# Perceiver layer on one Trainium2 core: tail products in two fp32r parts, set-up over more banks, the last group's rest in two token parts, the context's lower parts made by POOL

## Chip, cores and metric

One core of one Trainium2 chip runs the whole program in one launch. The metric is the device time of that launch in microseconds, the median of several runs.

## The reference, cut to what matters

64 batches of 32 queries (256 wide) look at 257 context rows (192 wide) with 16 heads of 64; then a self-attention of 16 heads of 16 over the 32 queries of a batch, then a gated feed-forward whose mixing takes the row before. All three are residual.

```python
x = x + xattn(layernorm(x), ctx)      # its own LN inside; q = xn@Wq, k,v = ctx@Wkv; softmax; @Wo + bo
x = x + attn(layernorm(x))            # LN; qkv = h@W_qkv + b; softmax over 32 keys; @W_proj + b
x = x + ffn(layernorm(x))             # xr, xk mix x and the row before; sigmoid(xr@Wr.T) * (relu(xk@Wk.T)**2 @ Wv.T)
```

## The kernel before

**Groups.** The 64 batches go in 8 groups of 8 (256 tokens, two tiles of 128). A group's work has three kinds. *Pre* work (XT, Q0 to Q3, K0 to K11) makes, for the next group, the queries already multiplied by the key weights (`qk_h`, `qk_l`, `qk_t`), so that scores are taken against the context itself. *Batch* work is the cross-attention of one batch `j`. *Post* work (OT0, OT1, WO0, WO1, T2, QT, KT, SC, VR, PT, PV, T4, PJ, T3, FR, FK, FV) is everything behind the cross-attention, for the group before.

**Batch work.** CT transposes the context on TensorE into `aux`; ACT rounds it to an upper part `cT_h` (fp32r) and DVE subtracts to get the lower part `cT_l`. S0 to S3 (L661) are four score tiles of five fp32r products each. DVE masks them and takes the row extremes (L1142), ACT makes the exponentials and their sums (L928), DVE the reciprocals (R0, R1, L1148), POOL normalises (N0, N1, L491). P0 and P1 transpose the probabilities (L670) into `probT`; ACT copies them to `prT` (L937), then to the fp32r upper part `prT_h` (U0, U1, L945), and POOL subtracts to get `prT_l` (L0, L1, L356). CU (ACT, L952) and CL (DVE, L348) make the same two parts of the context's first 128 channels, `c_h` and `c_l`. AC (`weigh`, L685 to L695) multiplies: the context's last 64 channels, the tail, in plain fp32 from `prT` and `cx_in` (four matmuls of 256 columns, L685), and the first 128 channels in six fp32r matmuls of 512 columns (L691, L692, L695) into `ac_main`. It waits for `prT` before the tail, for `prT_h` and `c_l` before the first four of the six, and for `prT_l` before the last two. ACT copies `ac_main` to `acm`, DVE `ac_tail` to `act_`.

**Order.** Each engine runs through a list written out by hand (`PE_ORDER`, `ACT_ORDER`, `DVE_ORDER`, `POOL_ORDER`), the same for all groups; what a group does not have is left out by `stream`. An engine issues its list in order, so a wait holds all that stands behind it. After the last group the `*_CLOSING` lists do the post work of group 7, all 256 tokens in each step, over eight PSUM banks.

**Set-up.** SP loads x, all of Wq (1 MB), the key weights, the context's last rows, small columns, the three feed-forward weights, the mask, four contexts and the rest. TensorE transposes x (XT), then the key weights (WK0 to WK3) and the feed-forward weights (F0 to F2) between Q0 to Q3, and then K0 to K10 over two pairs of PSUM banks, each waiting for the split before the last; the first score waits for 10 of the 12 splits. POOL's first work waits for all eight weight loads, and ACT's first for all seven small loads.

**Layer norm** (`layer_norm` on DVE) is a chain of small instructions linked by a semaphore: statistics, their sum, a seed by integer shift, three Newton steps of three links each, and the normalising pass.

## Time and profile before

| | us |
|---|---|
| median of 3 runs (902.51 to 904.21) | 902.88 |
| the profiled execution | 905.87 |
| its span, first to last instruction | 903.4 |
| PE busy of the span | 822.6 |
| DVE, ACT, POOL busy | 579.5, 549.5, 430.7 |

A busy time is the union of an engine's instructions. TensorE's are pipelined with modelled ends, so the distance between two starts tells more of its rate than the duration of one. In timeline rows the columns are the start in us from the span's start, the duration in us, engine, line, operation, what is written and read, shape and count; in brackets the engine's idle time before it and what ended it.

### The profile page before, as it was taken

What the parts mean: (1) busy time and instruction counts of PE and PEld (TensorE: products, weight loads), DVE (VectorE), ACT (ScalarE), POOL (GpSimd) and SP (SyncE); (2) the same over time, 40 slices, a digit from 0 to 9 for tenths busy, and PEclk for the clock granted to TensorE, in tenths of its full rate; (3) what the DMA queues carried; (4) which work ended last, traced back from release to release, by engine and by line L of the source; (5) the groups of instructions that cost most, each with busy time, mean ns of one, the idle gap of its engine ahead of it and who ended that gap; (6) DMA issues with size and microseconds to landing.
All of it is one profiled execution on the core that took longest, in us unless ns stands there. A gap on an engine that the chain in (4) does not pass through costs nothing.

```text
span 903.4 us, 20097 instructions
## 1 busy us (share of the span) xinstructions
PE 822.6 (91%) x7414; PEld 641.3 (71%) x7414; DVE 579.5 (64%) x1674; ACT 549.5 (61%) x1338; POOL 430.7 (48%) x661
## 2 busy tenths in 40 slices
PE   5699989998999989998999989998999999897653
PEld 3487758785878758786878768785878768684532
DVE  2553475769576775778576775778576756682344
ACT  1566865688467865677467865677467864673111
POOL 1036733755256723755266724755266724764001
PEclk9889999999999999999999999999999999999767
DMA  7301110001000110102010110002000110000000
GB/s 208 123 12 48 25 48 13 25 25 50 22 25 25 28 56 12 26 24 64 9 25 25 36 48 13 25 24 71 1 25 25 37 36 13 25 12 24 1 1 12
DMA packets 49232, 30.49 MB, mean 34 GB/s; under 512 B 22896, under 2 KB 48304, under 8 KB 49136
## 3 DMA queue, kind: packets, MB, share of 16 engines
q1 hardware_dynamic: 49136, 29.22, 11.9%
q8 instruction: 59, 0.97, 0.5%
q14 instruction: 37, 0.30, 0.1%
HBM read 26.85 MB, written 2.10 MB: 32 GB/s over the span
## 4 chain that ended last, share of the span: by engine, by line
PE 67%; DVE 14%; issue 7%; POOL 6%; ACT 5%; SPq 1%; DMA 1%; POOLq 0%; DVEq 0%; ACTq 0%
PE score L661 15%; PE post L755 5%; PE pre L573 5%; DVE qk_t L1123 5%; PE probT L670 4%; PE ac_tail L685 4%; POOL prT_l L356 4%; PE post L764 3%; DVE qk_l L1118 3%; PE ac_main L691 3%; PE ac_main L695 3%; PE aux L624 2%; PE ac_main L692 2%; PE post L738 2%; PE post L744 2%
## 5 line engine op out<-in xcount | busy, mean ns | idle before, releaser
L491 POOL TENSOR_SCALAR pr<-pr,rsum,poison 128x257 f32<-128x257 f32 x256 | 166.6, 660 | 233.6 <-DVE rsum L1148 233.5
L356 POOL TENSOR_TENSOR prT_l<-prT,prT_h 128x512 fp32r<-128x512 f32 x128 | 169.1, 1324 | 126.6 <-ACT prT_h L945 126.6
L928 ACT ACTIVATE pr<-sm,nmx 128x257 f32<-128x257 f32 x256 | 129.8, 509 | 83.8 <-DVE nmx L1142 83.4
L1142 DVE CUSTOM_DVE_ANT_0 sm<-score,mbias 128x257 f32<-128x257 f32 x256 | 106.2, 422 | 85.4 <-PE score L661 68.5
L937 ACT ACTIVATE prT<-probT 128x512 f32<-128x512 f32 x128 | 75.6, 590 | 44.9 <-PE probT L670 44.5
L661 PE MATMUL score<-cT_h,qk_h 128*128 128x258 f32 x256 | 89.6, 350 | 13.2 <-DVE qk_t L1123 12.9
L945 ACT ACTIVATE prT_h<-prT 128x512 fp32r<-128x512 f32 x128 | 80.7, 630 | 1.1
L670 PE MATMUL probT<-ident,pr 128*128 128x128 f32 x512 | 77.7, 274 | 3.4 <-POOL pr L491 2.6
L661 PE MATMUL score<-cT_h,qk_t 128*128 128x258 f32 x256 | 73.5, 287 | 0.0
L661 PE MATMUL score<-cT_l,qk_h 128*128 128x258 f32 x256 | 73.1, 285 | 0.0
L661 PE MATMUL score<-cT_h,qk_l 128*128 128x258 f32 x256 | 73.1, 285 | 0.0
L685 PE MATMUL ac_tail<-prT,cx_in 128*64 128x256 f32 x512 | 70.2, 395 | 3.0 <-ACT prT L937 2.3
L661 PE MATMUL score<-cT_l,qk_t 128*128 128x258 f32 x256 | 72.9, 285 | 0.0
L670 PEld LDWEIGHTS probT<-ident,pr 128*128 128x128 f32 x512 | 60.1, 140 | 14.1 <-POOL pr L491 7.2
L661 PEld LDWEIGHTS score<-cT_h,qk_h 128*128 128x128 f32 x256 | 48.8, 191 | 25.2 <-DVE qk_t L1123 12.5
L573 PE MATMUL pre<-xnT,wq 128*128 128x256 f32 x256 | 64.0, 395 | 0.5 <-ACT xnT L891 0.5
L1132 DVE TENSOR_TENSOR cT_l<-aux,cT_h 128x512 fp32r<-128x512 f32 x64 | 44.0, 688 | 27.3 <-ACT cT_h L920 27.0
L691 PE MATMUL ac_main<-prT_h,c_h 128*128 128x512 f32 x128 | 57.8, 451 | 0.0
L573 PEld LDWEIGHTS pre<-xnT,wq 128*128 128x128 f32 x256 | 48.4, 199 | 6.4 <-issue 0.7
L1148 DVE RECIPROCAL rsum<-ssum 128x2 f32<-128x2 f32 x128 | 20.5, 160 | 49.2 <-ACT pr L928 49.1
L685 PEld LDWEIGHTS ac_tail<-prT,cx_in 128*64 128x64 f32 x512 | 31.8, 137 | 28.0 <-issue 11.0
L692 PE MATMUL ac_main<-prT_h,c_l 128*128 128x512 f32 x128 | 51.0, 398 | 0.0
(260 smaller groups left out, 2024.5 us busy)
## 6 DMA issues: line engine op xcount, KB each, us to landing
cx_in<-in_ctx_dram SPq DMA_DIRECT2D x64, 192.0 KB, 2.4
cx_in<-in_ctx_dram SPq DMA_DIRECT2D x64, 64.0 KB, 2.3
xn<-in_x_dram SPq DMA_DIRECT2D x8, 256.0 KB, 3.4
xb<-in_x_dram SPq DMA_DIRECT2D x8, 256.0 KB, 3.5
out_dram<-yo SPq DMA_DIRECT2D x8, 256.0 KB, 2.7
wq<-in_L_xattn_Wq_dram SPq DMA_DIRECT2D x1, 1024.0 KB, 5.1
wo<-in_L_xattn_Wo_dram SPq DMA_DIRECT2D x1, 1024.0 KB, 7.6
wqkv<-in_L_attn_W_qkv_dram SPq DMA_DIRECT2D x1, 768.0 KB, 8.8
```

Of the source, the lines that this page charges most:

```text
L356: eng.tensor_tensor(prT_l[:, :, cut], prT[:, :, cut], prT_h[:, :, cut], ALU.subtract).then_inc(prob_lower, 1)
L491: last = pool.tensor_scalar(p, p, rsum[:, j % 2, t:t + 1], poison[:, 0:1], ALU.mult, ALU.mult)
L573: last = pe.matmul(pre[:, i * TOK:(i + 1) * TOK], wq[:, k, (2 * n + i) * P:(2 * n + i + 1) * P], xnT[:, k, :], start=(k == 0), stop=(k == 1))
L661: last = pe.matmul(score[t % 2][:, 0:NK + 1], q[:, j, tile], c, start=(i == 0), stop=(i == len(products) - 1))
L670: last = pe.transpose(probT[:, m * 256 + i * P:m * 256 + (i + 1) * P], pr[j % 2][:, 2 * half + i, m * P:(m + 1) * P], ident[:])
L685: pe.matmul(ac_tail[r * 64:r * 64 + 64, 0:TOK], cx_in[j % NCTX][:, m, P:DC], by_pair[:, :, r, :], start=(m == 0), stop=(m == 1))
L691: pe.matmul(ac_main[:], c_h[j % 2][:, m, :], prT_h[:, m, :], start=(m == 0), stop=False)
L692: pe.matmul(ac_main[:], c_l[j % 2][:, m, :], prT_h[:, m, :], start=False, stop=False)
L928: act.activation(pr[j % 2][:, t, :], sm[:, t % 2, :], ACT.Exp, bias=nmx[:, j % 2, t:t + 1], scale=-1.0, accum_out=ssum[:, j % 2, t:t + 1]) ...
L937: act.activation(prT[:, :, half * 256:(half + 1) * 256], probT[:].rearrange("p (m c) -> p m c", m=2), ACT.Copy).then_inc(probT_copied, 1)
L945: act.activation(prT_h[:, :, cut], prT[:, :, cut], ACT.Copy).then_inc(prob_upper, 1)
L1142: dve.tensor_tensor_reduce(sm[:, t % 2, :], score[t % 2][:, 0:NK], mbias[:], DH ** -0.5, BIG, ALU.add, ALU.min, nmx[:, j % 2, t:t + 1]).th ...
```

## The change

**AC.** `c_h` and `c_l` become one tile `c_hl` of 128 x 2 x 384: upper part of the first 128 channels, then upper and lower parts of the tail side by side (TAILS, 128 wide), then the lower part of the first 128. The tail is no longer plain fp32: four fp32r matmuls of 512 columns with TAILS as stationary operand write `ac_tail`, its rows 0 to 63 for the upper and 64 to 127 for the lower part. The wait for `prT` alone goes; all of AC waits for `prT_h` and `c_lower`, and the two last pairs for `prT_l`. ACT copies rows 64 to 127 to `act_low` ahead of its copy of `ac_main`; DVE adds the halves in two instructions. CL, now two subtractions, is made by POOL. CU rounds 192 columns a row where it took 128. `prT` is written again once `prT_l` is made, not once AC is done; that wait moves to `prT_h`.

```diff
 def weigh(g, j):
-    pe.wait_ge(probT_copied, n)
-    for m in range(2):
-        by_pair = prT[:, m, :].rearrange("p (n r x) -> p n r x", r=2, x=2 * NQ)
-        for r in range(2):
-            pe.matmul(ac_tail[r * 64:r * 64 + 64, 0:TOK], cx_in[j % NCTX][:, m, P:DC], by_pair[:, :, r, :],
-                      start=(m == 0), stop=(m == 1))
     pe.wait_ge(c_lower, g * GB + j + 1)
     pe.wait_ge(prob_upper, n)
+    c = c_hl[j % 2]
     for m in range(2):
-        pe.matmul(ac_main[:], c_h[j % 2][:, m, :], prT_h[:, m, :], start=(m == 0), stop=False)
-        pe.matmul(ac_main[:], c_l[j % 2][:, m, :], prT_h[:, m, :], start=False, stop=False)
+        pe.matmul(ac_main[:], c[:, m, UPPER], prT_h[:, m, :], start=(m == 0), stop=False)
+        pe.matmul(ac_main[:], c[:, m, LOWER], prT_h[:, m, :], start=False, stop=False)
+        pe.matmul(ac_tail[:], c[:, m, TAILS], prT_h[:, m, :], start=(m == 0), stop=False)
     pe.wait_ge(prob_lower, n)
     for m in range(2):
-        last = pe.matmul(ac_main[:], c_h[j % 2][:, m, :], prT_l[:, m, :], start=False, stop=(m == 1))
+        pe.matmul(ac_main[:], c[:, m, UPPER], prT_l[:, m, :], start=False, stop=(m == 1))
+        last = pe.matmul(ac_tail[:], c[:, m, TAILS], prT_l[:, m, :], start=False, stop=(m == 1))
 def context_lower(eng, g, j):
-    eng.tensor_tensor(c_l[j % 2][:], cx_in[j % NCTX][:, :, 0:P], c_h[j % 2][:], ALU.subtract).then_inc(c_lower, 1)
+    eng.tensor_tensor(c[:, :, DC:2 * P], src[:, :, P:DC], c[:, :, P:DC], ALU.subtract)
+    eng.tensor_tensor(c[:, :, LOWER], src[:, :, 0:P], c[:, :, UPPER], ALU.subtract).then_inc(c_lower, 1)
-LOWER_ON_DVE = ("CL",)
+LOWER_ON_DVE = ()
 def weighed(g, j):   # ACT
+    after(act, act_copied, g * GB + j)
+    act.activation(act_low[:], ac_tail[64:128], ACT.Copy).then_inc(tail_lower, 1)
     act.activation(acm[...], ac_main[...], ACT.Copy).then_inc(acm_copied, 1)
 def weighed(g, j):   # DVE
-    dve.wait_ge(ac_done, g * GB + j + 1)
-    dve.tensor_copy(act_[...], ac_tail[:, 0:TOK]...).then_inc(act_copied, 1)
+    dve.wait_ge(tail_lower, g * GB + j + 1)
+    for r in range(2):
+        last = dve.tensor_tensor(own, upper[:, :, r], lower[:, :, r], ALU.add)
+    last.then_inc(act_copied, 1)
```

**Orders.** Each engine gets three lists: for group 0, for groups 1 to 6, and for group 7 with its own rest. The middle ones differ in places only; AC stands on average a little later behind its P1.

```diff
 PE_ORDER = (
-    "S0:0 S1:0 CT:1 OT0 S2:0 S3:0 OT1 LV0 S0:1 P0:0 CT:2 LV1 WO0 XT S1:1 WO1 S2:1 S3:1 P1:0 CT:3 Q0 S0:2 AC:0 T2 S1:2 "
...
-    "S1:7 S2:7 FK AC:5 S3:7 P0:6 FV P1:6 K0 K2 AC:6 P0:7 K4 P1:7 K6 LT K8 AC:7 CT:0 K10").split()
+    "S0:0 CT:1 S1:0 OT0 S2:0 S3:0 OT1 CT:2 LV0 P0:0 LV1 S0:1 WO0 S1:1 P1:0 WO1 S2:1 XT AC:0 S3:1 Q0 CT:3 S0:2 T2 S1:2 "
...
+    "S1:7 FR S2:7 P0:6 FK AC:5 S3:7 P1:6 FV K0 K2 AC:6 P0:7 LT K4 P1:7 K6 CT:0 K8 AC:7 K10").split()
 DVE_ORDER = (
...
-    "CT:7 AC:4 S1:6 S2:6 R1:5 M1 S3:6 CL:5 S0:7 R0:6 FR CL:6 S1:7 R1:6 S2:7 SG AC:5 R0:7 S3:7 FV K0 CL:7 K1 R1:7 K2 K3 "
-    "AC:6 K4 K5 LT K6 K7 K8 K9 CT:0 AC:7 K10 K11").split()
+    "R0:7 R1:7 AC:5 K0 K1 K2 K3 LT K4 K5 AC:6 K6 CT:0 K7 K8 K9 K10 K11 AC:7").split()
 POOL_ORDER = (
...
+    "CT:1 XB CL:0 CL:1 N0:0 CT:2 N1:0 L0:0 L1:0 N0:1 N1:1 CT:3 X1 N0:2 CL:2 L0:1 L1:1 N1:2 CT:4 N0:3 L0:2 L1:2 N1:3 W0 W1 "
...
```

**Last group.** The post work of group 7 is done for tokens 0 to 127 (names with .0) and 128 to 255 (.1) apart, the first part in two PSUM banks and the second in six, with a second set of scratch tiles in `wq`. OT0.0, OT1.0 and WO.0 stand ahead of AC:7. The output is stored in two parts.

```diff
-PE_CLOSING = (
-    "OT0 OT1 WO0 WO1 T2 KT QT SC0 VR SC1 PT0 PT1 PV T4 PJ T3 FR FK FV").split()
+PE_LAST = (
...
+    "S2:7 S3:7 P1:6 AC:5 FR FK P0:7 AC:6 FV OT0.0 P1:7 OT1.0 WO.0 LT.1 AC:7 OT0.1 T2.0 OT1.1 QT.0 KT.0 WO.1 SC.0 VR.0 "
+    "T2.1 QT.1 KT.1 SC.1 VR.1 PT.0 PV.0 T4.0 PJ.0 PT.1 PV.1 T4.1 PJ.1 T3.0 T3.1 FR.0 FK.0 FR.1 FV.0 FK.1 FV.1").split()
+DVE_LAST = (
...
+    "B1.0 B2.0 B3.0 B4.0 B5.0 LT.1 B6.0 AC:7 B7.0 B8.0 B9.0 B10.0 B11.0 KM.0 WO.1 B0.1 B1.1 B2.1 B3.1 B4.1 B5.1 B6.1 B7.1 "
+    "B8.1 B9.1 B10.1 B11.1 SC.0 VR.0 KM.1 SM.0 SC.1 VR.1 SM.1 PJ.0 C0.0 C1.0 C2.0 C3.0 C4.0 C5.0 PJ.1 C6.0 C0.1 C7.0 C8.0 "
+    "C1.1 C9.0 C2.1 C10.0 C3.1 C11.0 C4.1 C5.1 C6.1 C7.1 C8.1 C9.1 C10.1 C11.1 M1.0 FR.0 M1.1 SG.0 FR.1 FV.0 SG.1 FV.1").split()
```

**Set-up.** SP loads the two small columns that XT needs and the key weights ahead of Wq, and Wq in two halves; the feed-forward weights come later and are transposed in group 0 (F0 to F2). K0 to K11 of group 0 (H0 to H11) run over four pairs of banks; score tile 0 waits for 4 of the splits, tile 1 for 6, tile 2 for 10, tile 3 for 12. Waits for all weights and all small loads move to where they are used. A two-column ACT copy stands ahead of the first real one.

```diff
-SETUP = "WK0 Q0 WK1 F0 Q1 WK2 F1 Q2 WK3 F2 Q3".split()
+SETUP = "WK0 WK1 XT WK2 WK3 Q0 LEFT Q1 CT0".split()
+PE_FIRST = (
+    "H0 G2 H2 S0:0 H4 H6 CT:1 G3 H8 H10 S1:0 S2:0 LV0 S3:0 CT:2 S0:1 P0:0 S1:1 LV1 P1:0 S2:1 S3:1 CT:3 F0 S0:2 S1:2 S2:2 "
...
+QK_SETUP_BANKS = [(score[0], score[1]), (post, probT), (ac_main, ac_tail), (post, probT), (ac_main, ac_tail), (post, pre)]
+FIRST_USE_0 = {0: 4, 1: 6, 2: 10, 3: 12}
```

**Layer norm.** -0.5 times the variance is made once, so a Newton step is two links (one `scalar_tensor_tensor` for each token tile, then one for both) and each link is a job of its own in DVE's list.

## Rows read from the trace of the kernel before

**Rows 1.** The page's first part: busy us, share of the span, instructions.
```profile
PE 822.6 (91%) x7414; PEld 641.3 (71%) x7414; DVE 579.5 (64%) x1674; ACT 549.5 (61%) x1338; POOL 430.7 (48%) x661
```

**Rows 2.** Windows, us: length, busy of PE, PEld, DVE, ACT, POOL, clock, DMA.
```profile
0.00:50.00 50.00, 31.73 (x189) 22.79 (x190) 21.99 (x69) 18.71 (x37) 3.34 (x17) 0.90 0.51 149
427.00:528.00 101.00, 98.36 (x921) 77.61 (x921) 71.94 (x208) 67.67 (x167) 54.06 (x81) 1.00 0.12 30
730.00:826.00 96.00, 88.09 (x785) 68.66 (x785) 57.75 (x176) 55.98 (x145) 54.68 (x79) 0.98 0.08 23
826.00:904.00 78.00, 44.67 (x420) 32.42 (x420) 28.71 (x66) 12.82 (x25) 5.79 (x6) 0.76 0.01 4
```

**Rows 3.** PE's timeline: the first score of group 1 and of group 7.
```profile
123.71 0.36 PE L661 MATMUL score<-cT_h,qk_h 128*128 128x258 f32 x1 [1.37 <-DVE qk_t L1123]
...
730.55 0.36 PE L661 MATMUL score<-cT_h,qk_h 128*128 128x258 f32 x1 [1.37 <-DVE qk_t L1123]
```

**Rows 4.** PE's timeline: one AC and the score behind it.
```profile
405.55 1.08 PE L685 MATMUL ac_tail<-prT,cx_in 128*64 128x256 f32 x8
406.56 0.50 PE L691 MATMUL ac_main<-prT_h,c_h 128*128 128x512 f32 x1
406.90 0.39 PE L692 MATMUL ac_main<-prT_h,c_l 128*128 128x512 f32 x1
...
408.06 0.28 PE L661 MATMUL score<-cT_h,qk_h 128*128 128x258 f32 x1
```

**Rows 5.** Lines by form: count, busy us, mean ns; idle before.
```profile
L348 DVE TENSOR_TENSOR c_l<-cx_in,c_h 128x256 fp32r<-128x256 f32 x64 | 34.6, 551 | 0.3
L1123 DVE TENSOR_TENSOR qk_t<-score,qk_t 64x512 fp32r<-64x512 f32 x32 | 22.0, 689 | 1.7 <-ACT qk_t L911 1.0
L1160 DVE COPY act_<-ac_tail 128x256 f32<-128x256 f32 x64 | 26.5, 414 | 10.4 <-PE ac_main L695 10.0
L911 ACT ACTIVATE qk_t<-score 64x512 fp32r<-64x512 f32 x32 | 18.9, 592 | 2.2 <-PE score L610 1.9
L356 POOL TENSOR_TENSOR prT_l<-prT,prT_h 128x512 fp32r<-128x512 f32 x128 | 169.1, 1324 | 126.6 <-ACT prT_h L945 126.6
L506 POOL TENSOR_TENSOR xb<-xb,bo_row 128x256 f32<-128x256 f32 x16 | 11.3, 729 | 0.0
```

**Rows 6.** Timeline of the stretch K0 to K10, a group's last 16 us.
```profile
514.86 1.52 DVE L348 TENSOR_TENSOR c_l<-cx_in,c_h 128x256 fp32r<-128x256 f32 x1
...
528.26 0.36 PE L661 MATMUL score<-cT_h,qk_h 128*128 128x258 f32 x1 [1.35 <-DVE qk_t L1123]
```

**Rows 7.** Timeline of the set-up.
```profile
7.93 1.08 PE L556 MATMUL pre<-ident,xn 128*128 128x128 f32 x4 [7.93 <-DVE xn L1099]
...
12.77 1.02 ACT L891 ACTIVATE xnT<-pre,cols 128x256 f32<-128x256 f32 x2 [2.38 <-DMA bcol<-in_L_attn_b_qkv_dram]
...
13.93 3.75 PE L573 MATMUL pre<-xnT,wq 128*128 128x256 f32 x8 [0.55 <-ACT xnT L891]
...
44.98 0.55 PE L661 MATMUL score<-cT_h,qk_h 128*128 128x258 f32 x1 [3.40 <-DVE qk_t L1123]
```

**Rows 8.** Timeline behind the last AC, from its copy to the store.
```profile
825.95 0.60 ACT L956 ACTIVATE acm<-ac_main 128x512 f32<-128x512 f32 x1 [3.78 <-PE ac_main L695]
...
835.54 3.69 PE L755 MATMUL ac_tail<-wo,qT 128*128 128x256 f32 x16 [1.29 <-ACT qT L988]
...
847.65 1.12 PE L556 MATMUL score<-ident,hn 128*128 128x128 f32 x4 [4.97 <-DVE hn L1099]
...
867.60 1.05 POOL L517 TENSOR_TENSOR sc<-sc,rs 128x512 f32<-128x512 f32 x1 [22.97 <-DVE rs L1211]
...
880.24 0.69 DVE L1223 TENSOR_TENSOR x<-post,xb 128x512 f32<-128x512 f32 x1 [11.28 <-PE post L799]
...
894.77 3.35 DVE L1250 RECIPROCAL sc<-sc 128x512 f32<-128x512 f32 x1
...
900.89 0.38 SPq L414 DMA_DIRECT2D out_dram<-yo  x1
```

888 lines of the change are left out of this document (503 added, 385 removed), and 40 rows, old and new, of tables (ACT_FIRST, ACT_LAST, ACT_ORDER, DVE_FIRST).

## The prediction

> **What bounds the kernel now.** I read the page's busy times first: TensorE is busy for 91% of the span, no other engine for more than 64% [rows 1]. The windows say where the rest lies. A middle group holds TensorE for 98.4 of its 101 us, with DVE at 71.9, ACT at 67.7 and POOL at 54.1 [rows 2]; there TensorE's own work is the time, and the groups repeat to a hundredth: from 123.71 to 730.55 six of them take 101.14 each [rows 3]. The two ends are another matter. In the first 50 us TensorE is busy for 31.7; behind the last AC it is busy for 44.7 of 78 at a mean clock of 0.76 [rows 2]. Three sizes follow: a start of 123.7 us up to group 1, six groups of 101.1, a last group of 95.4 up to the end of its last AC at 825.9, and a rest of 77.5 up to 903.4 [rows 3, 8].
>
> **AC.** The fp32 tail takes 1.01 us (405.55 to 406.56) and the six fp32r matmuls 1.50: the first 0.34, the other five 0.23 each [rows 4]. The new AC is ten such matmuls, 2.31 at 0.23, or 2.42 with a first one of 0.34. The dearer first is what the turn from fp32 to fp32r costs, and there is one such turn before and after. So 2.51 becomes 2.31 to 2.42; an fp32 piece ahead is also overlapped by the turn, so I take 0.2 saved (bounds 0.09 and 0.28). That is **1.6 us a group**, 13 in all.
>
> The other engines pay. ACT copies 64x512 more (0.59 [rows 5]) and rounds 192 columns for 128 (some 0.1); that is 8 x 0.69 = 5.5, so 73 of 100. DVE loses CL (8 x 0.55 = 4.4) and has two additions for one copy, each like that copy's 0.41 (so 8 x 0.41 = 3.3 more), and stays near 71. POOL gains CL: 128x256 at 0.73 as its additions, and the 128x128 part, of which no row tells: between nothing and the same 0.73; 1.32 for 512 elements and 0.73 for 256 [rows 5] lead on to 0.43 for 128, which I take. So 1.16 a batch, 9.3 a group (5.8 to 11.7), 63 of 100. None passes TensorE, so in the sum these cost nothing; their cover is TensorE's queue, and the first rival below says what happens if it is gone.
>
> What is queued behind the moved wait: AC now starts when `prT_h` is made, where the tail needed `prT` alone, and what lies between AC's start and the wait for `prT_l` shrinks from 1.01 + 0.96 to 1.39 us. But `prT` may be rewritten without waiting for the last AC, and the lists put AC:0 some 4.5 us of TensorE work behind P1:0 where it had 2.8, while copy, rounding and subtraction take 0.6 + 0.6 + 1.3 (the last in [rows 5]). I cost it at zero, with 0.4 us per AC as the other end.
>
> **The stretch of K0 to K10.** At every group's end the first score waits 1.35 us for DVE's last split [rows 6], and DVE's `c_l` in that stretch takes 1.52 us, against a mean of 0.55, beside POOL's `prT_l`. It leaves DVE's chain there, one extra addition (0.41) comes in: 1.1 us of the wait go. I take **1.0 us a group**; nothing at worst, 2 at best with the other waits of that stretch. The GPSIMD Engine Reference of the Trainium skill (Specifications) says that POOL's SBUF interface is shared with VectorE and that contention comes with two-SBUF-input instructions of DVE; by that rule the collision goes for good, since the new additions have one operand in PSUM. By the row alone it could move to another DVE instruction, and the 1.0 would be zero, 7 us in all.
>
> **Middle groups:** 101.1 - 1.6 - 1.0 = 98.5, six times 2.6 is **-15.6** (between 0 and -27).
>
> **Set-up and group 0.** x is normalised by 7.9, and then `xnT` waits for small loads until 12.77, 2.38 us of it for the DMA alone [rows 7]. The new order has the two columns and the key weights ahead of Wq's megabyte. The key weights should be there near 7, so WK0, WK1 and XT run from 7 to 11, where TensorE had XT and then stood idle, and Q0 starts near 13.5 as before (13.93 [rows 7]), but behind four WK instead of one. F0 to F2 leave (2 us at the low clock) and return in group 0 at full clock (1.3). Two Q's at 3.75 [rows 7] bring H0 to 21.5. DVE's 12 splits are 16 instructions of 0.69 [rows 5], 11 us; with a mask, CT:1 and some 3 us of waits between they end near 37. Before, the tenth came at 44.98, after a wait of 3.40 [rows 7], and the last two 1.4 later, at 46.4: 9 us, and 2 more as score tiles, CT:1 and LV0 now run between the K's, where they followed. From -11, plus 1.3 for F0 to F2, -1.6 for AC, -1.0 for the stretch at the end: **-12** (between -6 and -16). The waits for weights stand at LV0, near 37; the loads land before 31 now and the bytes are the same, so they cost nothing.
>
> **Last group up to its last AC.** It has no next queries to make, and TensorE is busy for 88.1 of 96 [rows 2]. AC saves 1.6; OT0.0, OT1.0 and WO.0 come in. OT takes 7.7 us (9.6 from 825.95 to 835.54, less 0.6 and 1.3 for the copies [rows 8]); on half the columns 3.8 if the columns set the time, 7.7 if the instructions do. I take 4.6, near the columns. WO.0 takes 3.6, as one of the two. 88.1 - 1.6 + 8.2 = 94.7, and some waits remain: **0** (between -3 and +5).
>
> **The rest.** The second token part sets the end; I walk the milestones [rows 8] with halved work:
> - 825.95 to 835.54, 9.6: now the tail's copy and additions first (+1.0), half of OT (4.6), T2.0, QT.0 and KT.0 in between (2.4), copies: 8.6.
> - to 847.65, 12.1: one WO (3.6), not two, one addition, a layer norm of 3.0 where it was 4.4 (12.1 less two WO and 0.4; now one tile, and 11 links for 14): 7.1.
> - to 867.60, 20.0: T2, hT, QT, KT on half the columns 3.5, KM 2.4, then DVE's own queue: SM.0, SC.1, VR.1, SM.1, some 5.4 at 0.69 for 512 and 0.41 for 256 elements [rows 5]: 11.3. DVE is the bound here, as it carries both parts.
> - to 880.24, 12.6: one POOL product (1.05), one PT, PV, T4, PJ behind those of part 0: 6.8.
> - to 894.77, 14.5: layer norm 3.0 with 1.5 of the other part's links, T3, mixing, FR: 10.3.
> - to 900.89, 6.1: the reciprocal of 3.35 is halved to 1.7, the last product and sum as well: 3.0. Then the store, 2.5.
>
> Together 49.6. I add 5 for the clock and for in-order queues, since the chip had TensorE at 0.76 here and more but shorter gaps may leave it there: 54.5, **-23** (between -15 and -28).
>
> **Sum:** 903.4 - 12 - 15.6 - 0 - 23 = 852.8 for the span, 855.3 for the execution (2.5 around the span). The profiled execution lies 3.0 above the median of the runs shown, so the median should be **852 us**, 5.6% less.
>
> **Rivals.**
> 1. *POOL in the way, slower than before.* CL stands in POOL's list ahead of N and L, which P and AC wait for, in order. If all of it (1.1 us) lay on the path of each batch, 8.8 us a group, seven groups 62, the sum would be 852 + 62 = 914; it decides from 0.9 us a batch. For it: POOL is 1.3 to 1.8 times slower than DVE at this shape [rows 5], and with TensorE at 98% every new wait counts. Against: POOL stands idle 47 of 101 us, and its L waits for ACT's `prT_h` for most of that [rows 5]. The same reference's table (Engine selection) says not to give GpSimd an elementwise instruction of two inputs, some 2x slower than VectorE there, which speaks against this part of the change; twice DVE's 0.41 and as much in proportion for the tail would make CL an estimated 1.3, POOL 65 of 100, and the point of decision nearer, the sum the same. 3%.
> 2. *The middle groups gain nothing.* The later start of AC and ACT's 0.6 us before each `acm` copy give back 2.6 us a group as new waits: 852 + 15.6 = 868. For it: 0.3 us per AC is enough. Against: AC stands later. 17%.
> 3. *The clock stays low at both ends.* Work in short pieces leaves TensorE at 1.2 GHz: some 20 us of its work in the rest take 6 more, the start 4 more: 862. For it: both halves of the rest still wait for DVE. 15%.
> 4. *More goes.* TensorE's idle time left in a middle group (2.6 [rows 2], less the 1.0 taken) goes as well, and AC saves 0.28 (0.6 a group): 96.3 a group, 13 us more: 839. For it: the lists are new for the new work. 12%.
> 5. *The change does nothing in the middle and little at the ends*, as both are bound by loads and DVE: within 0.2% of before, 1%.
> The forecast itself has 52%.
>
> **How the numbers follow.** Cases 2 to 4 reach 839 to 868; the unknowns of the terms move the forecast by some 10 either way. I take 838 to 872 as the range that holds the time 8 times in 10. 0.2% is about what a measurement of this kernel tells from no change. Faster by more has 0.96, same 0.01, slower 0.03.
>
> **What would show it.** In the profile after: AC in ten matmuls 2.3 to 2.4 us from start to start; the first scores of groups 1 and 7 at 111.7 and 702.7, 98.5 apart per group; the wait ahead of each group's first score below 0.5 us; the fourth score of batch 0 near 39; POOL busy for some 63% of a group; 54 to 55 us from the last AC to the end. I am wrong if TensorE waits for `prT_h`, `prT_l` or `pr` at most ACs (rival 1 or 2), or if the rest takes over 62 us, which would put the error in DVE's queue between the two parts.

## The result and the profile after

The changed kernel takes 894.94 us (median of 9 runs, 892.30 to 898.48) where the kernel before, in the same comparison, takes 901.89: a ratio of 0.9926, with a 95% interval of 0.9905 to 0.9947. That is 0.7% faster. I had said 852 us, in a range of 838 to 872, so the sign was right and the size far off. (One profiled execution of an experiment, that of e1_setup_order, ran at a granted clock of 0.85 throughout and took 948.66 us; it is left out of that kernel's time.)

Its profiled execution spans 890.3 us. First the page's first part, to be read against [rows 1]; columns as there.

```profile
PE 808.1 (91%) x7279; PEld 658.7 (74%) x7279; DVE 587.8 (66%) x1729; ACT 600.1 (67%) x1423; POOL 480.0 (54%) x792
```

TensorE lost 14.5 us of work, ACT and POOL gained some 50 each. The windows, to be read against [rows 2], show the stages. Columns: stretch, its length, busy time of PE, PEld, DVE, ACT and POOL with the instruction counts, clock, DMA share, GB/s.

```profile
0.00:50.00 50.00, 32.50 (x190) 20.99 (x191) 22.17 (x65) 17.59 (x37) 4.52 (x21) 0.90 0.52 149
427.00:527.00 100.00, 97.03 (x893) 80.15 (x891) 72.22 (x210) 73.92 (x175) 59.68 (x97) 1.00 0.12 31
724.32:836.27 111.95, 95.10 (x866) 77.72 (x866) 61.12 (x186) 63.10 (x156) 61.50 (x96) 0.98 0.08 21
836.27:890.29 54.02, 32.90 (x429) 25.66 (x428) 32.39 (x91) 15.64 (x42) 5.46 (x7) 0.86 0.02 6
```

A middle group still keeps TensorE busy 97% of the time. The last group, up to the end of its last AC, is 112 us long for 95 us of work. Next, the first scores of group 1, of a middle group and of group 7 in TensorE's timeline, the rows that answer to [rows 3] (start, length, instruction, and in brackets the idle time before it and what ended it).

```profile
124.55 0.39 PE L786 MATMUL score<-cT_h,qk_h 128*128 128x258 f32 x1
...
424.44 0.39 PE L786 MATMUL score<-cT_h,qk_h 128*128 128x258 f32 x1 [0.81 <-DVE qk_t L1270]
...
724.32 0.39 PE L786 MATMUL score<-cT_h,qk_h 128*128 128x258 f32 x1 [0.79 <-DVE qk_t L1270]
```

So six groups take (724.32 - 124.55) / 6 = 99.96 us each. One AC in the same view, with the score behind it, answers to [rows 4].

```profile
483.38 0.48 PE L812 MATMUL ac_main<-prT_h,c_hl 128*128 128x512 f32 x1
483.69 0.39 PE L813 MATMUL ac_main<-prT_h,c_hl 128*128 128x512 f32 x1
483.93 0.40 PE L814 MATMUL ac_tail<-prT_h,c_hl 128*128 128x512 f32 x1
...
485.76 0.28 PE L786 MATMUL score<-cT_h,qk_h 128*128 128x258 f32 x1
```

From 483.38 to 485.76 are 2.38 us: 0.31 for the first matmul and 0.23 for each of the nine others. And the lines by form of the whole span for the work that the other engines took over, to be read against [rows 5] (count, busy us, mean ns; idle before).

```profile
L419 POOL TENSOR_TENSOR c_hl<-cx_in,c_hl 128x128 fp32r<-128x128 f32 x64 | 29.6, 462 | 13.5 <-ACT c_hl L1073 13.4
L420 POOL TENSOR_TENSOR c_hl<-cx_in,c_hl 128x256 fp32r<-128x256 f32 x64 | 47.0, 734 | 0.0
L1079 ACT ACTIVATE act_low<-ac_tail 64x512 f32<-64x512 f32 x64 | 38.2, 596 | 23.0 <-PE ac_tail L818 21.7
L1302 DVE TENSOR_TENSOR act_<-ac_tail,act_low 64x256 f32<-64x256 f32 x128 | 52.7, 412 | 4.6 <-ACT act_low L1079 3.7
```

The four stretches of the prediction's sum, in us:

| stretch | before | forecast | after | off by |
|---|---|---|---|---|
| start to the first score of group 1 | 123.7 | -12 | 124.55 (+0.8) | 12.8 |
| six middle groups | 606.8 | -15.6 | 599.8 (-7.1) | 8.5 |
| last group to the end of its last AC | 95.4 | 0 | 112.0 (+16.6) | 16.6 |
| the rest | 77.5 | -23 | 54.0 (-23.5) | -0.5 |
| sum | 903.4 | -50.6 | 890.3 (-13.1) | 37.5 |

The 13.1 us of the last line are more than the 6.7 us that the ratio gives. The 903.4 belong to an execution of 905.87 us, slower than all nine of this comparison, and the 890.3 to the fastest of its nine (892.30). The start is one part that moves from one execution to the next: in e5_before_cl_pool below, whose lists are those of before up to there, the first score comes at 40.91 where it is at 44.98 in before, as TensorE waits 0.96 and not 2.50 us for its first load (`acm`), and the Q matmuls behind it reach their full pitch sooner. So the +0.8 of the first line is known to some 4 us only, which does not make a -12 of it.

The rest came as forecast, the other three did not. The experiments take them one by one. All are held against the kernel before, run on the same chip beside them; stages come from one profiled execution of each.

### The profile page after: what moved, and what is told of

It reads as the page before. It is cut to its first block, busy times and chain, and to the rows that moved or that the text cites. A ratio compares the mean times of both kernels' runs of the same rounds, so it can differ in the third digit from the quotient of the medians.

```text
span 890.3 us, 20369 instructions
## 1 busy us (share of the span) xinstructions
PE 808.1 (91%) x7279; PEld 658.7 (74%) x7279; DVE 587.8 (66%) x1729; ACT 600.1 (67%) x1423; POOL 480.0 (54%) x792
## 4 chain that ended last, share of the span: by engine, by line
PE 66%; DVE 16%; ACT 6%; issue 6%; POOL 3%; SPq 1%; DMA 1%; DVEq 0%; POOLq 0%; ACTq 0%
PE score L786 14%; PE post L872 5%; DVE qk_t L1270 4%; PE pre L671 4%; PE probT L797 4%; PE post L881 3%; PE aux L730 2%; PE ac_main L812 2%; DVE qk_l L1265 2%; PE ac_main L817 2%; PE ac_tail L818 2%; PE ac_tail L814 2%; PE ac_main L813 2%; DVE kM L1350 2%; PE post L852 2%
## 5 line engine op out<-in xcount | busy, mean ns | idle before, releaser
L571 POOL TENSOR_SCALAR pr<-pr,rsum,poison 128x257 f32<-128x257 f32 x256 | 141.8, 564 | 157.7 <-DVE rsum L1295 157.6
L786 PE MATMUL score<-cT_h,qk_h 128*128 128x258 f32 x256 | 92.5, 362 | 19.1 <-DVE qk_t L1270 11.4
L786 PE MATMUL score<-cT_h,qk_l 128*128 128x258 f32 x256 | 72.7, 284 | 0.0
L786 PE MATMUL score<-cT_l,qk_t 128*128 128x258 f32 x256 | 72.7, 284 | 0.0
L812 PE MATMUL ac_main<-prT_h,c_hl 128*128 128x512 f32 x128 | 55.7, 435 | 4.0 <-POOL c_hl L420 2.6
L671 PE MATMUL pre<-xnT,wq 128*128 128x256 f32 x232 | 55.5, 382 | 0.6 <-ACT qT L1014 0.6
L1302 DVE TENSOR_TENSOR act_<-ac_tail,act_low 64x256 f32<-64x256 f32 x128 | 52.7, 412 | 4.6 <-ACT act_low L1079 3.7
L1079 ACT ACTIVATE act_low<-ac_tail 64x512 f32<-64x512 f32 x64 | 38.2, 596 | 23.0 <-PE ac_tail L818 21.7
L1039 ACT ACTIVATE cT_h<-aux 128x512 fp32r<-128x512 f32 x64 | 38.2, 597 | 21.8 <-PE aux L730 21.8
L817 PE MATMUL ac_main<-prT_l,c_hl 128*128 128x512 f32 x128 | 50.3, 393 | 1.0 <-POOL prT_l L428 1.0
L786 PEld LDWEIGHTS score<-cT_l,qk_h 128*128 128x128 f32 x256 | 49.0, 192 | 2.3
L872 PE MATMUL post<-wo,qT 128*128 128x256 f32 x224 | 50.6, 379 | 0.0
```

The lines of the kernel that those rows point to most:

```text
L571: last = pool.tensor_scalar(p, p, rsum[:, j % 2, t:t + 1], poison[:, 0:1], ALU.mult, ALU.mult)
L671: last = pe.matmul(bank[:, i * TOK:(i + 1) * TOK], wq[:, k, (2 * n + i) * P:(2 * n + i + 1) * P], xnT[:, k, :], start=(k == 0), stop=(k == 1))
L786: last = pe.matmul(score[t % 2][:, 0:NK + 1], q[:, j, tile], c, start=(i == 0), stop=(i == len(products) - 1))
L812: pe.matmul(ac_main[:], c[:, m, UPPER], prT_h[:, m, :], start=(m == 0), stop=False)
L817: pe.matmul(ac_main[:], c[:, m, UPPER], prT_l[:, m, :], start=False, stop=(m == 1))
L872: last = pe.matmul(bank[:, 0:DM], qT[:, k, w * P:(w + 1) * P], wo[:, k, :], start=(k == 0), stop=(k == NPAIR - 1))
```

## The experiments

### The order of the split stretch

Where did the set-up's 12 us go? The first H products stand where I had them (H0 at 21.50, forecast 21.5), but the fourth score of batch 0 comes at 48.77, not near 39. In the changed kernel's timeline two rows tell of it, TensorE's first score and ACT's copy of the context of batch 1.

```profile
29.95 0.58 PE L786 MATMUL score<-cT_h,qk_h 128*128 128x258 f32 x1 [4.41 <-DVE qk_t L1270]
```

```profile
35.88 0.60 ACT L1039 ACTIVATE cT_h<-aux 128x512 fp32r<-128x512 f32 x1 [7.41 <-PE aux L730]
```

TensorE's list has S0:0, which waits for four splits, ahead of H4 and H6, which could have run. ACT's list has CT:1 ahead of H4. CT:1 stands in TensorE's list behind H6, so ACT stands idle for 7.4 us although H4's products were ready 2.6 us before that ended (33.3), and DVE behind it stands for 6.6. Only this order was changed:

```diff
-PE_FIRST  "H0 G2 H2 S0:0 H4 H6 CT:1 G3 H8 H10 ..."
+PE_FIRST  "H0 G2 H2 H4 G3 CT:1 S0:0 H6 H8 H10 ..."
-ACT_FIRST "H0 H1 H2 G2 H3 CT:1 H4 H5 H6 G3 H7 ..."
+ACT_FIRST "H0 H1 G2 H2 H3 H4 H5 G3 CT:1 H6 H7 ..."
-DVE_FIRST "H0 H1 H2 H3 CT:1 H4 S0:0 H5 H6 ..."
+DVE_FIRST "H0 H1 H2 H3 H4 H5 CT:1 S0:0 H6 ..."
```

> Kernel after with only the hand-written order of the split stretch changed: the second products H4 ahead of the first score, ACT copies H4 and H5 ahead of the context of batch 1, DVE likewise. Theory 1 (the in-order queues cost the start its gain): TensorE stood 4.4 us ahead of the first score with H4 and H6 behind it, ACT stood 7.4 us for the context while H4's products were ready. Then the fourth score of batch 0 comes at 41 to 43 us instead of 48.8, group 1's first score at 117 to 119 instead of 124.6, and the kernel is 6 to 8 us shorter than after (about 888). Rival (DVE's splits and the low clock set the stretch, whatever the order): the fourth score stays within 1.5 us of 48.8 and the time within 2 us of after (893 to 897).

Measured: 888.00 us (three executions), ratio 0.9847 (0.9799 to 0.9895). In its profiled execution the fourth score comes at 41.66 and group 1's first score at 119.78. The same order in c1_both below, at a granted clock of 0.98, gives 41.10 and 117.20, both inside what theory 1 said. TensorE's first, second and fourth score in c1_both:

```profile
30.80 0.39 PE L788 MATMUL score<-cT_h,qk_h 128*128 128x258 f32 x1 [0.91 <-DVE qk_t L1272]
...
35.83 0.39 PE L788 MATMUL score<-cT_h,qk_h 128*128 128x258 f32 x1
...
41.10 0.36 PE L788 MATMUL score<-cT_h,qk_h 128*128 128x258 f32 x1
```

The idle time ahead of the first score falls from 4.41 to 0.91 and 7.7 us are gone by the fourth. So a few items in three in-order lists cost 7.4 us of the start (124.55 to 117.20), of the 12.8 by which the forecast missed it. The loads were in time for this: TensorE's first H product came at 21.50, as forecast.

### The last group: the early part, and the order

The last group has two new things: OT0.0, OT1.0 and WO.0 ahead of its last AC, and lists of its own. First the early part alone was moved behind AC:7, on all engines.

```diff
 PE_LAST
-"... P0:7 AC:6 FV OT0.0 P1:7 OT1.0 WO.0 LT.1 AC:7 OT0.1 ..."
+"... P0:7 AC:6 FV P1:7 LT.1 AC:7 OT0.0 OT1.0 WO.0 OT0.1 ..."
 DVE_LAST
-"... AC:6 WO.0 B0.0 B1.0 B2.0 B3.0 B4.0 B5.0 LT.1 B6.0 AC:7 B7.0 ..."
+"... AC:6 LT.1 AC:7 WO.0 B0.0 B1.0 B2.0 B3.0 B4.0 B5.0 B6.0 B7.0 ..."
```

> Kernel after with the first token part's OT0.0, OT1.0, WO.0 and the links B0.0 to B6.0 moved behind the last AC on all engines; nothing else. In after the last group up to its last AC takes 112.0 us and the rest 54.0. Theory (the early work only moved, its 8.6 us of TensorE lie on the path wherever they stand): the last group 103 to 104, the rest 61 to 63, sum within 1.5 us of after. Rival A (early work in the way of AC:6 and AC:7, adding waits): last group below 102, rest at most 60, 3 us or more shorter. Rival B (early work fills gaps): last group above 106, sum 3 us or more longer.

Measured: 901.76 us, 0.9995 (0.9977 to 1.0014). The last group shrinks by only 2.0, from 112.0 to 110.0, and the rest grows from 54.0 to 66.6. Rival B is right: the early part fills gaps and is worth 10.5 us between the two profiled executions, and some 6 by the ratios (0.9995 against 0.9926). Then the 17 us of gaps come from elsewhere, and the next kernel keeps the early part out and runs the group in the middle groups' order.

```diff
-PE_LAST = "S0:0 CT:1 S1:0 OT0 S2:0 OT1 S3:0 S0:1 CT:2 WO0 ..."
+PE_LAST = PE_ORDER without the jobs for a next group, LT as LT.0 LT.1, then the closing jobs
```

The same was done to the lists of ACT, DVE and POOL.

> As e2_no_early, but the batch part of the last group runs in the order written for the middle groups (less the jobs for a next group) on all four engines. Theory (the last group's own lists are what leaves TensorE waiting 17 us there, the middle order leaves about 3): last group 91 to 96 us, rest 61 to 63, the kernel 5 to 10 us shorter than e2_no_early and than after. Rival (what waits there is the missing work for a next group, so any order leaves the gaps): last group 102 to 104 as in e2_no_early, time the same.

Measured: 889.61 us, 0.9863 (0.9836 to 0.9891). Last group 96.8, rest 65.9. The rest is as long as in e2_no_early (66.6) and longer than the theory had it. The order alone is worth 13.2 us in the last group against e2_no_early, with the same instructions. TensorE's idle time there falls from 18.8 to 10.8 us, and its busy time from 91.1 to 86.0; the granted clock is 0.98 where it was 0.95, so the waits were in part paid for twice. The waits of TensorE (who waited for whom: us in total, times, longest) in the last group, first of the changed kernel:

```profile
PE probT L797 <- POOL pr L571: 3.0, 2, 2.1
PE score L786 <- DVE nmx L1289: 1.4, 2, 1.3
PE post L913 <- ACT kM L1136: 1.4, 1, 1.4
PE aux L730 <- DMA cx_in<-in_ctx_dram: 1.3, 2, 0.8
```

and of e3_last_mid:

```profile
PE ac_main L814 <- DVE act_ L1304: 3.7, 2, 2.0
PE post L647 <- DVE hn L1240: 1.9, 2, 1.0
PE aux L737 <- DVE spread L1312: 1.3, 1, 1.3
```

In the changed kernel there are eighteen such rows, of which the four largest are shown, for every kind of work. Probabilities, scores, contexts and post jobs all come a little late, which fits lists that are ordered badly from start to end. With the middle order there are ten rows, of which three are shown: the waits for POOL's `pr`, `prT_l` and `c_hl` and for the DMA are gone, that for the row extremes `nmx` falls from 1.4 to 0.3, and 5.0 of what is left stand in the last 11 us of the group, behind DVE.

Then the early part was put back into this order.

```diff
 PE_LAST (middle order)
-"... P1:6 FV AC:6 P0:7 LT.0 LT.1 P1:7 CT:0 AC:7 OT0.0 OT1.0 WO.0 ..."
+"... S1:7 LT.0 ... P1:6 FV OT0.0 AC:6 OT1.0 P0:7 WO.0 P1:7 LT.1 CT:0 AC:7 ..."
```

> As e3_last_mid (the last group's batch part in the middle groups' order), with the first token part's OT0.0, OT1.0, WO.0 and B0.0 to B6.0 put back among its last batches: OT0.0 and OT1.0 around AC:6, WO.0 behind P0:7. In e3 the last group took 96.8 us and the rest 65.9. Theory (the early part fills the last group's gaps, in e2 against after it brought 8 us net, and the order was what cost): last group 100 to 103, rest 54 to 56, the kernel 6 to 9 us shorter than e3, about 882. Rival (OT0.0, OT1.0 now delay AC:6 and AC:7 by what they take and their waits; no gap is left in the middle order): last group 105 or more, time as e3.

Measured: 889.72 us, 0.9833 (0.9810 to 0.9856). The last group takes 101.1 as the theory had it, but the rest 62.2 and not 54 to 56. So nothing clear is gained on e3: 0.9833 against 0.9863, with intervals that overlap. POOL's and DVE's timelines show why:

```profile
822.24 1.29 POOL L430 TENSOR_TENSOR prT_l<-prT,prT_h 128x512 fp32r<-128x512 f32 x1 [3.14 <-ACT prT_h L1068]
823.49 1.44 POOL L593 TENSOR_TENSOR xb<-xb,bo_row 128x256 f32<-128x256 f32 x2
```

```profile
825.02 0.42 DVE L1328 TENSOR_TENSOR x<-pre,xb 128x256 f32<-128x256 f32 x1 [9.70 <-issue]
...
827.03 1.16 DVE L1312 TENSOR_TENSOR spread<-aux,seqm 32x128 f32<-32x128 f32 x4
828.22 0.16 DVE L1249 SCALAR_TENSOR_TENSOR lw<-lw 128x1 f32<-128x1 f32 x1
828.30 0.84 DVE L1304 TENSOR_TENSOR act_<-ac_tail,act_low 64x256 f32<-64x256 f32 x2
```

POOL makes `xb` behind the last `prT_l`; DVE's addition for the first part waits for it, 9.7 us idle; and `spread` and the last AC's additions, for which the second part's OT waits, stand behind that addition. Again no engine is busy and a list holds it up.

### Both ends together, and the end mended

c1_both is e8_mid_early with the split stretch of e1_setup_order.

> e8_mid_early together with the order of e1_setup_order. Theory (the two ends don't touch): both gains add, e1's fourth score at 41 to 42 and group 1's first score at 117 to 119.8, then six groups of 99.9, last group and rest as in e8_mid_early: 6 us shorter than e8, about 876. Rival (group 0 gives the start's gain back, as it waits for weights or other engines there): group 1's first score at 122 or later and the time that of e8.

Measured: 880.01 us, 0.9728 (0.9707 to 0.9748). Group 1's first score comes at 117.20, the groups take 99.95, last group and rest 101.2 and 62.4 as in e8. The two ends do not touch: 9.7 us less than e8 by the medians and 6.5 by the profiled spans, of which 6.8 lie ahead of group 1; 6 were expected. c2_both mends the lists at the end of the last group:

```diff
 POOL_LAST "... L0:7
-L1:7 XB.0
+XB.0 L1:7
 DVE_LAST
-"... AC:6 WO.0 B0.0 B1.0 B2.0 B3.0 B4.0 B5.0 LT.1 B6.0 CT:0 AC:7 ..."
+"... AC:6 LT.1 WO.0 B0.0 B1.0 B2.0 B3.0 AC:7 B4.0 B5.0 B6.0 CT:0 ..."
 PE_LAST
-"... FV OT0.0 AC:6 OT1.0 P0:7 WO.0 P1:7 LT.1 CT:0 AC:7 ..."
+"... FV AC:6 OT0.0 P0:7 OT1.0 P1:7 WO.0 LT.1 CT:0 AC:7 ..."
```

ACT's list follows TensorE's.

> c1_both with the end of the last group mended: in the rest of e8 and c1 the second OT waits behind DVE's x addition for the first part, which waited for POOL's xb behind the last prT_l, with the last AC's additions and the spread queued behind it (last group and rest 101.2 and 62.2 us, where after has 112.0 and 54.0). Here POOL makes XB.0 before the last prT_l, DVE makes the spread ahead of that addition and the last AC's additions after four links of the norm, WO.0 stands behind P1:7 and OT1.0 behind P0:7. Theory: last group 100 to 102, rest 54 to 57, the kernel 5 to 8 us shorter than c1, 872 to 875. Rival (the second part's end is set by DVE's and ACT's work on the first part wherever its start lies): rest 60 or more, 878 or more.

Measured: 875.53 us, 0.9706 (0.9674 to 0.9738). Its windows of the last group and the rest:

```profile
716.01:818.76 102.75, 94.01 (x866) 77.57 (x866) 58.26 (x183) 63.30 (x156) 60.89 (x96) 0.98 0.09 23
818.76:873.87 55.11, 34.05 (x428) 27.02 (x428) 32.42 (x94) 15.56 (x42) 5.64 (x8) 0.83 0.02 6
```

The rest falls from 62.4 to 55.1 and the last group grows from 101.2 to 102.8, both from one profiled execution of each. The ratios do not tell this kernel from c1_both (0.9706 against 0.9728, the intervals overlap), so the 5 to 8 us expected from this step are not shown as a time. It beats the kernel before by 2.9% and the changed one by 2.2%, with the instructions of the changed one in another order. Its span of 873.9 is 21.1 us above my 852.8: 4.7 in the start (116.4 against 111.7), 8.4 in the middle groups, 7.4 in the last group and 0.6 in the rest.

One more list was tried in the first group. There TensorE waits 1.6 us in two ACs for `c_hl`, which POOL makes late although it stands idle for 17.8 us before.

```diff
 POOL_FIRST
-"CT:1 N0:0 CT:2 N1:0 L0:0 N0:1 N1:1 CL:0 L1:0 CL:1 CT:3 ..."
+"CT:1 CL:0 N0:0 CT:2 N1:0 L0:0 N0:1 CL:1 N1:1 L1:0 CT:3 ..."
```

> c2_both with POOL's list of the first group changed alone: CL:0 (0.46 and 0.72 us) ahead of N0:0, where POOL had stood idle for 17.8 us, and CL:1 behind N0:1, in place of both behind N1:1. In c2 POOL makes CL:0 at 51.87, and the first AC waits 0.94 us for it (1.6 in two ACs of the group). Theory (in the first group CL stands in the way of AC, rival 1 of the prediction on a small scale): these waits go, group 1's first score from 116.4 to 114.5 to 115.5, the kernel 1 to 2 us shorter. Rival (the next wait, for the rounded probabilities or for prT_l, takes their place): 116 or later, no difference.

Measured: 875.04 us, 0.9703 (0.9677 to 0.9728), no difference from c2_both. Group 1's first score stands at 116.80, so the rival holds. The waits of TensorE from 38 to 124 us in c3_pool_first:

```profile
PE aux L732 <- DMA cx_in<-in_ctx_dram: 2.4, 2, 1.7
...
PE ac_main L814 <- POOL c_hl L422: 0.6, 1, 0.6
```

The wait for `c_hl` falls from 1.6 to 0.6, and the one for the next contexts' DMA rises from 1.0 to 2.4.

### The AC alone, in the new lists

The middle groups gave 7.1 us of 15.6. Is the AC worth less than the 0.2 us that I took? e9_fp32_tail puts the old tail and the six fp32r matmuls back on TensorE and leaves everything else. The old tail reads a constant tile in the place of `prT`, so the kernel leaves the attention's tail out, and its tail waits for nothing. That does not favour it in the middle groups: no AC there waits, in the kernels before and after either.

```diff
+for m in range(2):
+    by_pair = wq[:, m, 0:512].rearrange("p (n r x) -> p n r x", r=2, x=2 * NQ)
+    for r in range(2):
+        pe.matmul(ac_tail[r * 64:r * 64 + 64, 0:TOK], cx_in[j % NCTX][:, m, P:DC], by_pair[:, :, r, :], ...)
 pe.wait_ge(c_lower, g * GB + j + 1)
...
-    pe.matmul(ac_tail[:], c[:, m, TAILS], prT_h[:, m, :], start=(m == 0), stop=False)
...
-    last = pe.matmul(ac_tail[:], c[:, m, TAILS], prT_l[:, m, :], start=False, stop=(m == 1))
```

> Kernel after with the AC of before on TensorE alone: the tail as four fp32 matmuls of 256 columns ahead of six fp32r matmuls, in place of the ten; ACT, DVE and POOL keep their new work and all lists stay. The fp32 tail takes a constant tile as moving operand, so the tail's sums are not the attention's (a changed part of the computation), the shapes are before's. Theory (the new AC is worth what its matmuls take less, nothing else in the middle groups changed for the better): pitch of an AC back from 2.38 to about 2.50, middle groups from 99.95 to 100.9 to 101.3, the kernel 8 to 11 us slower than after. Rival 1 (the prediction's 0.2 an AC): 101.5. Rival 2 (TensorE's idle time takes it up, since other engines set the pace with ACT at 74 and the rounding waited for): 99.9 to 100.4.

Measured: 904.19 us, 1.0017 (0.9996 to 1.0038), against 0.9926 for the changed kernel. A middle group takes 101.44 us where it was 99.96: 1.48 a group, 0.185 an AC. That is rival 1, the prediction's number, not my theory of 0.12. The old AC itself takes 1.01 + 1.49 = 2.50 here and the new one 2.38, so a third of the gain lies outside the AC's own row, in waits or turns beside it; where exactly is open.

So with the AC worth 1.5 us a group and the groups only 1.2 shorter than before, everything else in the change costs a middle group 0.3 us. That is a sum of parts with opposite signs, as TensorE's waits in one group show. Before (427.12 to 528.26) there are four, 2.60 us, all in the stretch from K0 to the first score; the last of them is in [rows 6], and these are the others:

```profile
518.70 0.66 PE L670 MATMUL probT<-ident,pr 128*128 128x128 f32 x4 [0.19 <-POOL pr L491]
519.95 0.43 PE L601 MATMUL pre<-qT,nwk 64*64 64x256 f32 x2 [0.59 <-DVE qk_t L1123]
...
521.72 1.09 PE L610 MATMUL score<-qT,nwkt 64*64 64x256 f32 x16 [0.47 <-DVE qk_l L1118]
```

After (424.44 to 524.36) there are five, 2.67 us:

```profile
426.77 0.65 PE L852 MATMUL post<-acm,wvn 128*64 128x256 f32 x4 [0.42 <-issue]
...
482.35 0.36 PE L786 MATMUL score<-cT_h,qk_h 128*128 128x258 f32 x1 [0.63 <-POOL cT_l L553]
...
514.95 0.27 PE L735 MATMUL aux<-ident,lastp 128*32 128x128 f32 x1 [0.33 <-POOL lastp L580]
...
518.94 1.09 PE L716 MATMUL score<-qT,nwkt 64*64 64x256 f32 x16 [0.50 <-DVE qk_l L1265]
...
524.36 0.39 PE L786 MATMUL score<-cT_h,qk_h 128*128 128x258 f32 x1 [0.79 <-DVE qk_t L1270]
```

In the stretch from K0 on the waits fall from 2.60 to 1.62, which is the 1.0 that I took for it. But two new ones, 1.05 together, stand further ahead. The larger is POOL's: it makes `c_hl` (1.18 us for both parts) just ahead of two small casts that a score tile waits for.

```profile
481.22 0.72 POOL L420 TENSOR_TENSOR c_hl<-cx_in,c_hl 128x256 fp32r<-128x256 f32 x1
...
482.02 0.18 POOL L553 CAST cT_l<-left_l 128x2 fp32r<-128x2 f32 x1
```

TensorE's busy time in these groups is 98.36 us before, 98.78 in e9 and 96.97 after. So the AC took 1.8 of work off it, of which 0.3 came back as idle time, and the rest of the change, the new order with it, added 0.4 of work; what in the new order costs this was not tried.

### The parts of the change in the old kernel

e5_before_cl_pool changes the kernel before in one way: POOL makes `c_l` (128x256).

```diff
-LOWER_ON_DVE = ("CL",)
+LOWER_ON_DVE = ()
 POOL_ORDER "... N1:0
-L0:0
+CL:0 L0:0
```

and so on for each batch.

> Kernel before with only one part of the change: the lower part of the context (128x256) made by POOL, each just ahead of the first probability half of the same batch in POOL's list, not by DVE. Theory (the prediction's term: the wait of 1.35 us ahead of each group's first score is DVE's chain with c_l of 1.5 us in it): the wait falls to 0.5 or less and a middle group from 101.14 to 100.1 to 100.4, time about 896. Rival (POOL's 0.72 us ahead of N and L is paid by the probabilities' and AC's waits, or the collision moves to another DVE instruction): middle group 101.0 to 103, time the same or up to 915.

Measured: 908.02 us, 1.0047 (1.0028 to 1.0067): slower, by 0.5%. The middle groups take (729.79 - 119.74) / 6 = 101.68, half a microsecond more. The wait that I had blamed on `c_l` stays. TensorE's waits in one group (424.76 to 526.66) are four, of which three are shown; the fourth, for `qk_l`, is 0.47 as before:

```profile
471.52 1.07 PE L772 MATMUL post<-kM,q2T 128*32 128x256 f32 x16 [0.98 <-DVE kM L1195]
...
497.02 0.63 PE L557 MATMUL post<-ident,hn 128*128 128x128 f32 x4 [0.60 <-DVE hn L1100]
...
526.66 0.36 PE L662 MATMUL score<-cT_h,qk_h 128*128 128x258 f32 x1 [1.38 <-DVE qk_t L1124]
```

The last wait is 1.38 where it was 1.35. What is gone are the two short waits of before, 0.19 for `pr` and 0.59 for the `qk_t` that DVE makes in one unbroken chain behind `c_l`. From K0 (512.49 before, 511.63 here) to the next group's first score it takes 15.03 us where it took 15.77. So the move of `c_l` is worth 0.7 us in this stretch. It is not worth more because the wait of 1.35 hangs on a later piece: TensorE's K8, ACT's four copies (2.4), DVE's four subtractions (2.8) and, in this kernel, `cT_l` of the next batch, whose end at 424.66 lies 0.10 ahead of that group's first score at 424.76. The rest of the 1.5 us turned into idle time of DVE, which waits 0.31 us twice for ACT's copies where `c_l` stood. One of the two rows:

```profile
515.47 1.39 DVE L1124 TENSOR_TENSOR qk_t<-pre,qk_t 64x512 fp32r<-64x512 f32 x2 [0.31 <-ACT qk_t L912]
```

Against the 0.7 stand the waits of 0.98 and 0.60 (0.3 in some groups) in post work further ahead, which the kernel before does not have. POOL's list is the only one that gained work here, so they come by way of POOL, and they make the group longer on balance. The last group is 3.0 us longer too (98.4 against 95.4).

e4_before_new_ac gives the kernel before only the new AC, with both lower parts by DVE. DVE's AC jobs were moved back where ACT's copy of the low half would else come after them.

```diff
-act.activation(c_h[j % 2][:], cx_in[j % NCTX][:, :, 0:P], ACT.Copy)
+act.activation(c_hl[j % 2][:, :, 0:DC], cx_in[j % NCTX][:, :, 0:DC], ACT.Copy)
+act.activation(act_low[:], ac_tail[64:128], ACT.Copy).then_inc(tail_lower, 1)
-DVE_ORDER "... S1:2 AC:0 S2:2 ... R1:2 CL:2 AC:1 SC0 ..."
+DVE_ORDER "... S1:2 S2:2 AC:0 ... R1:2 CL:2 SC0 ... CT:4 AC:1 ..."
```

> Kernel before with only the new AC: tail products in fp32r with the upper and lower parts, ACT copies the low half out and DVE adds, lower parts of the context still by DVE, DVE's AC job moved back in its list as far as ACT's copy demands; all else as before. Theory (an AC saves 0.12 us by the ten matmuls of after, 2.36 to 2.40 from start to start against 2.50, and the six DVE and ACT additions are hidden): middle groups 101.14 - 1.0 = 100.1, all eight 8 us less, about 895. Rival (the later start of AC, which now needs the rounded probabilities, and ACT's copy ahead of acm turn into waits when the lists are not made for it): middle groups 101 to 103, time 900 to 917.

Measured: 1020.21 us, 1.1309 (1.1270 to 1.1347). A middle group takes 115.8 us, beyond the rival's 103. e7_before_ac_pool is the same with both lower parts on POOL, at the places of e5.

> Kernel before with the new AC and the context's lower parts on POOL, in before's order (e4_before_new_ac with the parts moved from DVE to POOL). e4 had 115.9 us a middle group against 101.14. Theory (in e4 the lists, not an engine's load, cost the 15 us: AC waits for prT_h and prT_l, and the in-order queues pass each wait on): moving the parts to POOL leaves the groups at 113 to 118. Rival (DVE's queue with the added work was what stood in the way, POOL frees it): 103 or less.

Measured: 1017.51 us, 1.1288 (1.1252 to 1.1323), 115.5 a group. DVE's busy time falls from 79.1 of 116 us to 74.7 of 115 and nothing follows, so it is not the load of `CL` on DVE. That it is the lists follows from the changed kernel, whose middle groups do the same AC work in 99.96 us with other lists (and the shorter layer norm, which was not tried apart). TensorE's waits in one group of e4_before_new_ac, from 365.7 to 481.66, begin with these two:

```profile
PE post L813 <- DVE kM L1240: 4.1, 1, 4.1
PE ac_main L693 <- POOL prT_l L359: 3.1, 2, 2.2
```

e6_after_cl_dve takes the lower parts from POOL in the changed kernel and gives them to DVE, in new places.

```diff
-LOWER_ON_DVE = ()
+LOWER_ON_DVE = ("CL",)
-POOL_ORDER "CT:1 XB CL:0 CL:1 N0:0 ..."
+POOL_ORDER "CT:1 XB N0:0 ..."
-DVE_ORDER "S0:0 A0 A1 S1:0 A2 A3 A4 CT:1 A5 A6 S2:0 ..."
+DVE_ORDER "S0:0 A0 A1 CL:0 S1:0 A2 A3 A4 CT:1 A5 A6 CL:1 S2:0 ..."
```

> Kernel after with the lower parts of the context (128x256 and 128x128, two instructions) given back to DVE, at the places of DVE's list where ACT's upper part is ready; POOL's list without them. Theory (DVE's instructions are what TensorE waits for, POOL has room: the move was worth the 0.5 us a group that the wait ahead of the first score fell): middle group 100.5 to 102 where after has 99.95, POOL down from 60 to 50, DVE up from 72 to 78. Rival (POOL's queue is what costs the middle groups in after, through waits for columns, c_hl and pr): middle group 98 to 99.5, kernel 4 us or more faster than after.

Measured: 989.73 us, 1.0935 (1.0897 to 1.0974), 112.6 a group; the theory had at most 102. DVE is busy for 65.1 of 100 us there, so again it is not load. This run says that the new lists are made for `CL` on POOL, and by itself it says nothing of which engine is the better place: my places in DVE's list are one choice of many. That question stays open. e5 answers it only for the old lists and its one place, where the move costs half a microsecond a group.

## Why the prediction was right or wrong

**The bound.** Right: a middle group is TensorE's work, and POOL, ACT and DVE rise to 59.7, 73.9 and 72.2 of 100 without becoming the bound (forecast 63, 73 and near 71).

**AC.** Right. 1.6 us a group forecast, 1.48 by e9. The row alone says less (0.12 an AC), the bounds 0.09 to 0.28 held both. The later start of AC cost nothing, as forecast: none of the 48 ACs of the middle groups waits.

**What the other engines pay: prices right, cost wrong.** The prices: 0.46 + 0.73 for `CL` on POOL (1.16 forecast for both), 0.596 for ACT's copy (0.59), 0.41 for each DVE addition. The Trainium skill (GPSIMD Engine Reference, Engine selection) has GpSimd some 2x slower than VectorE for elementwise work of two inputs. This case shows 0.73 against the 0.55 that `c_l` took on DVE on average [rows 5], and against its median of 416 ns, as the summary of this tile in the kernel before has it (duration in ns, minimum, median and maximum):

```profile
L348 DVE TENSOR_TENSOR c_l<-cx_in,c_h x64: 403/416/1568, 50.0 to 815.0; 128x256 fp32r<-128x256 f32 x64
```

That is 1.8 times, so the trace agrees with the rule's size. Though POOL is idle for 40 of 100 us there, the work was not free. "None passes TensorE, so in the sum these cost nothing" is the step that failed in the middle groups: it compares busy times and does not ask what waits behind the new work in POOL's list. There `c_hl` stands ahead of the casts for a score, 0.63 us a group, and 0.42 more of idle time is new elsewhere. (A small slip: twice 0.41 and half as much for the tail are 1.2 for CL and 64 of 100, not 1.3 and 65.)

**The stretch of K0 to K10: size right, way wrong.** "It leaves DVE's chain there ... 1.1 us of the wait go." The waits of the stretch fell by 0.98 in the changed kernel, against 1.0 taken. But the `c_l` of 1.52 us [rows 6] was early in the chain, and the wait of 1.35 came 13 us later, behind a piece that starts when TensorE issues K8. e5 parts the two: without `c_l` on DVE that wait stays (1.38), and two others, 2 to 4 us behind `c_l`, go (0.78). In the kernel after the wait ahead of the first score is 0.79 to 0.81, with CT:0 now ahead of K7 in DVE's list; which part of the 0.98 comes from the order and which from `c_l` is not shown, so that the size fits is in part luck. The same page of the Trainium skill (Specifications) says that POOL and VectorE contend when a DVE instruction has two SBUF inputs. The trace agrees: this `c_l` starts at 514.86, beside POOL's `prT_l` of 514.82 to 516.10, and ends at 516.38, where its median is 0.42.

**Middle groups together.** Forecast 1.6 + 1.0 = 2.6 less, measured 1.2. TensorE's work fell by 1.4 and not 1.6 (the AC -1.8, the rest of the change +0.4), and its idle time did not fall: -0.98 in the stretch, +1.05 ahead of it, and 0.1 in gaps too short for a row. New waits in the middle are what rival 2 described, though it had AC's later start as their cause; the 0.63 behind `CL` is rival 1 on a small scale. Over six groups the miss is 8.5 of the 37.5 us.

**Set-up: failed.** The step was "DVE's 12 splits are 16 instructions of 0.69 ... with a mask, CT:1 and some 3 us of waits between they end near 37". It added up DVE's work and never walked the three lists against each other, in which S0:0 stands ahead of H4 and CT:1 ahead of H4's copy. H0 came at 21.50 as forecast, the last split near 45.4, not 37. With the order mended (c2_both) the fourth score comes at 40.5 against the 39 forecast. What lies behind it in group 0 was off too: 75.8 us from the fourth score to group 1, where before took 74.5 and I had 72.7. TensorE's busy time fell by 1.6 there (AC's gain is in it, and F0 to F2), and its idle time grew from 5.8 to 8.7 us. c3 shows that the largest of its waits, taken away, is replaced by another; more of this is not settled.

**Last group: failed, the largest miss.** "88.1 - 1.6 + 8.2 = 94.7, and some waits remain: 0." TensorE's work was right, 95.1. The 7 us of idle time that 95.4 had before became 17. I read the group as the sum of TensorE's work and took it that waits would shrink as work was added. The lists written for this group do not keep TensorE fed, which e3 shows against e2: 13.2 us by order alone. With the middle order and the same work it takes 101.1 (e8: busy 92.4, idle 8.7), 5.7 above the forecast and just outside its bound of +5. So even in a good order the waits were not below those of before, and the forecast had left 0.7 us for them. The early part itself was as good as the change could hope: it costs 2.0 us ahead of the last AC and saves 12.6 behind.

**The rest: right**, with two steps short and the allowance filling them. From the last AC's copy at 836.31 the second part's milestones in the changed kernel came after 8.2 us (WO.1; forecast 8.6), 7.3 (the transposes behind its norm; 7.1), 13.2 (POOL's product; 11.3), 6.6 (the PJ addition; 6.8), 13.5 (the reciprocal; 10.3), 3.1 (the last sum; 3.0) and 2.2 (the end; 2.5). The two stages in which DVE carries both parts are 5.1 us longer together, and 5 was the allowance made for clock and in-order queues. That it fits so well is luck. Whether DVE's queue or the clock made them longer was not parted: from 872 to 882, inside the stage of 13.5, the granted clock is 0.50. Three rows of DVE's and POOL's timelines:

```profile
871.55 0.42 DVE L1380 TENSOR_TENSOR x<-score,xb 128x256 f32<-128x256 f32 x1 [2.64 <-PE score L921]
...
885.04 1.75 DVE L1411 RECIPROCAL sc<-sc 128x256 f32<-128x256 f32 x1
```

```profile
864.97 1.05 POOL L602 TENSOR_TENSOR sc<-sc,rs 128x512 f32<-128x512 f32 x1 [3.74 <-DVE rs L1367]
```

**The rivals and the range.** Rival 1 priced POOL in each batch's path at 0.9 to 1.1 us; in after TensorE waits for `c_hl` 2.6 us in the whole span. Rival 3 (the clock) was wrong for the rest: 0.86 on average over it, against 0.76 before [rows 2], though it is low in parts. In the start the clock is 0.90 in both and 1.00 in c2_both; so it is higher where the lists leave less idle time. No rival held that a hand-written order could be bad at the very places for which it was written anew. In a kernel whose lists were changed in nearly every place that was the largest unknown, and e4 shows how large: 15 us a group when work changes and lists do not. The range of 34 us had nothing for it.

## What to carry to other kernels

When a change rewrites hand-made instruction orders, the price of its operations is the smaller half of the forecast: walk each engine's list against the others at the places where a waiting item stands ahead of one that is ready, and keep a case for a bad order with a size taken from the kernel's own idle time. A long instruction in a chain is worth what the waits behind it lose, so follow each of them back step by step; here 1.5 us were worth 0.7, at two short waits 2 to 4 us behind, and nothing at the long wait 13 us later. Work given to an engine that is idle for 40% is not free either: look at what stands behind it in that engine's list. When a stage gets worse with less work in it, try the order of a stage that is known to run well: it cost one experiment and gave 13 us.

## What the runs showed that I had not expected

- Replacing the fp32 tail by fp32r matmuls is worth 0.185 us an AC by the groups' length and only 0.12 by the AC's own rows (2.50 to 2.38). TensorE's busy time differs by 0.23 an AC. So something outside the AC's own row takes longer with the fp32 tail; which instruction was not found.
- The first of ten fp32r matmuls behind fp32 transposes took 0.31 us from start to start, the others 0.23; before it was 0.34 behind the fp32 tail [rows 4].
- POOL's normalisation (128x257, 256 of them) took 660 ns on average before, 564 after and 574 in e6, but 644 in e5 and 639 in e7, which have the old lists. So its length goes with the order of the work beside it, not with who makes `c_l`; which neighbour it is was not tried.
- Where TensorE stood idle 4.4 us ahead of the first score, the granted clock fell to the lower of its two levels, 1.2 GHz, and the work behind it ran at twice its pitch: the pieces of H4 and H6 were 0.42 us apart, where they are 0.21 apart in c1_both. A wait in a list there was paid for twice. The windows of those stretches, first of the changed kernel, then of c1_both:

```profile
30.00:36.00 6.00, 6.00 (x43) 3.91 (x44) 0.00 (x0) 0.12 (x1) 0.00 (x0) 0.54 0.02 5
```

```profile
28.00:42.00 14.00, 10.26 (x89) 7.09 (x88) 11.92 (x25) 9.09 (x19) 0.00 (x0) 1.00 0.11 38
```
